# First attention: scores at the end of TensorE's step, the fourth probability copy and the queries on VectorE, GpSimd's step in another order with the lists one step on

## The reference

```python
x = x + cross_attention(n(x), ctx, ctx, mask)   # 16 heads of 16; keys and values from ctx; then layer norm with gamma, beta
x = x + mixture_of_experts(n(x))                # 8 experts, each row goes to its best 2
```

## Time and profile before

| | us |
|---|---|
| median of 3 runs | 970.35 |
| lowest and highest run | 966.97, 971.49 |
| the profiled execution | 968.65 |
| its span, first to last instruction | 966.7 |
| mean granted TensorE clock | 0.971 |
| busy over the span: PE, DVE, ACT, POOL | 863.4, 600.0, 467.1, 391.7 |

### The profile page before, as it was taken

One profiled execution on the slowest core, in us unless ns is written; L12 is line 12 of the kernel. 1 busy time (PEld: TensorE's weight loads), 2 busy tenths in 40 slices (PEclk: granted clock), 3 DMA queues, 4 the chain that ended last, 5 costly groups with the idle time before them and its releaser, 6 DMA issues. The chain is left out here.

```text
span 966.7 us, 26667 instructions
## 1 busy us (share of the span) xinstructions
PE 863.4 (89%) x9044; PEld 729.9 (76%) x9045; DVE 600.0 (62%) x1484; ACT 467.1 (48%) x1194; POOL 391.7 (41%) x610
## 2 busy tenths in 40 slices
PE   4888888759999999998999899999999999779995
PEld 3676776439999999996556588888888887667784
DVE  3587887545555555542027567868668787459995
ACT  3788787412222222222343354445444454459895
POOL 4478886620000000006102346445564545436662
PEclk9999999979999999999999999999999999889998
DMA  6454656342433333316864696777676875212111
GB/s 165 118 164 155 196 159 214 136 165 76 137 95 93 108 95 98 98 35 211 287 197 148 144 180 151 157 148 167 142 158 143 163 157 119 64 41 63 58 59 45
DMA packets 190187, 128.27 MB, mean 133 GB/s; under 512 B 128544, under 2 KB 175648, under 8 KB 189984
## 3 DMA queue, kind: packets, MB, share of 16 engines
q1 hardware_dynamic: 155728, 93.72, 37.5%
q10 hardware_dynamic: 31312, 25.17, 9.1%
q0 software_dynamic: 3072, 8.39, 2.7%
HBM read 78.25 MB, written 48.99 MB: 132 GB/s over the span
## 5 line engine op out<-in xcount | busy, mean ns | idle before, releaser
L1745 ACT ACTIVATE c_pT<-c_T 128x512 f32<-128x512 f32 (+2 forms) x90 | 50.2, 595 | 104.9 <-PE c_T L1904 74.0
L1689 POOL TENSOR_TENSOR c_soft<-c_soft,c_share 128x616 f32<-128x616 f32 (+2 forms) x96 | 70.5, 764 | 63.3 <-DVE c_share L2158 61.8
L1699 POOL MEMSET d_round<- 128x1 f32 x1 | 0.1, 99 | 227.4 <-POOLq L970 227.4
L1080 ACT ACTIVATE b_rowsT<-b_RT 128x256 f32<-128x256 f32 x39 | 15.0, 385 | 157.8 <-PE b_RT L1122 157.8
L1194 DVE COPY b_w<-moe_w 128x1024 f32 x78 | 53.6, 688 | 53.0 <-issue 47.5
L1131 PEld LDWEIGHTS b_G<-b_rowsT,b_w 128*128 128x128 f32 x624 | 77.2, 195 | 4.5 <-DVE b_w L1194 2.4
L1131 PE MATMUL b_G<-b_rowsT,b_w 128*128 128x128 f32 x624 | 77.9, 279 | 1.7 <-DVE b_w L1194 1.1
L1208 DVE SCALAR_TENSOR_TENSOR b_hidT<-b_U,b_bias,b_gate 128x128 f32<-128x128 f32 x156 | 43.9, 344 | 55.6 <-PE b_U L1131 55.6
L1131 PE MATMUL b_U<-b_rowsT,b_w 128*128 128x128 f32 x624 | 76.8, 277 | 0.0
L1158 PE MATMUL b_Y<-moe_w,b_hidT 128*128 x312 | 73.9, 380 | 1.0 <-DVE b_out L1239 1.0
L1131 PEld LDWEIGHTS b_U<-b_rowsT,b_w 128*128 128x128 f32 x624 | 73.6, 194 | 0.0
(11 more groups left out here) (241 smaller groups left out, 2073.1 us busy)
## 6 DMA issues: line engine op xcount, KB each, us to landing
moe_w<-in_L_Wl SPq DMA_DIRECT2D x16, 512.0 KB
rel_windows<-c_relw ACTq DMA_DIRECT2D x28, 276.0 KB, 5.6
c_bias<-rel_windows SPq DMA_DIRECT2D x16, 462.0 KB, 4.9
prob_rows<-c_soft SPq DMA_DIRECT2D x16, 462.0 KB, 5.4
early<-in_L_early SPq DMA_DIRECT2D x16, 384.0 KB, 3.2
values<-c_pT ACTq DMA_DIRECT2D x22, 256.0 KB, 2.6
b_rows<-expert_lists SPq DMA_DIRECT2D x39, 128.0 KB, 2.2
expert_out<-b_out SPq DMA_DIRECT2D x39, 128.0 KB, 1.7
```

The lines of the kernel that those rows point to most:

```text
L1689: ins = nc.gpsimd.tensor_tensor(soft[p][:, hs, a:z], soft[p][:, hs, a:z], share[:, s, hs].unsqueeze(2).to_broadcast([P, HS, z - a]), ALU.mult)
L1745: nc.scalar.activation(dst, view(T[k]), ACT.Copy, **kw).then_inc(g["emptied"], 1)
```

## The change

ScalarE gives two things to VectorE: the query copies with their bias (now one `tensor_scalar` for each of two halves, add then multiply, so the scaled bias `bqs` goes), and the fourth probability copy (`last_probs`, with a semaphore `p3_sb` of its own). TensorE's step is reordered: places and transposes (now of b+1) first, `attention(b-2)` behind probability 0, the scores of b+1 at the end. VectorE's step is reordered too. On GpSimd `both_std` does two deviations in one pair of instructions while both batches exist; listing and scatter are now those of b-4, in the order listing, scatter, and masks come last. From step 16 on `std(2, .)` runs ahead of them.

```diff
-        names = ("... p_mm p_sb pv_mm ...
+        names = ("... p_mm p_sb p3_sb pv_mm ...
+        ALONE = NB - 5
...
+            def both_std(ahead, behind):
+
+                apart(pool, g["var1"], behind + 1)
+                apart(pool, g["var"], ahead + 1)
+                links[0].begin(ahead)
+                links[0](nc.gpsimd.tensor_tensor(rstd[:, 0:2, 0], agg[:, 0:2, 1], eps[:, :], ALU.add))
+                nc.gpsimd.tensor_tensor(rstd[:, 0:2, 1], rstd[:, 0:2, 0], shared["mhalf"][:, :].to_broadcast([P, 2]), ALU.pow)\
+                    .then_inc(g["rstd"], 1)
...
             def steps(b, i, p):
-                if there(b + 3):
+                if there(b + 3) and there(b - 2):
+                    both_std(b + 3, b - 2)
+                elif there(b + 3):
                     std(0, b + 3)
-                if there(b - 2):
+                elif there(b - 2):
                     std(1, b - 2)
-                if there(b + 2):
-                    masks(b + 2, i + 1, p)
-                if there(b - 2):
+                late = isinstance(b, int) and b >= NB
+                if there(b - 2) and late:
+                    std(2, b - 2)
+                if there(b - 4):
+                    listing(b - 4, p)
+                    if there(b - 1):
+                        apart(pool, g["p3_sb"], b)
+                    scatter(b - 4, p)
+                if there(b - 2) and not late:
                     std(2, b - 2)
                 if there(b - 1):
                     residual(b - 1, i - 1 + p, 1 - p)
-                if there(b - 3):
-                    if there(b - 1):
-                        apart(pool, g["p_sb"], 4 * (b - 1) + HPT)
-                    scatter(b - 3, 1 - p)
-                    listing(b - 3, 1 - p)
+                if there(b + 2):
+                    masks(b + 2, i + 1, p)
 
             by_batch(steps)(pool)
+            listing(NB - 1, 1)
+            scatter(NB - 1, 1)
...
ScalarE:
                 if there(b - 1):
-                    for k in range(2):
+                    for k in range(HPT - 1):
                         probs(b - 1, k)
                 if there(b - 3):
                     next_rows(b - 3)
-                if there(b - 1):
-                    for k in range(2, HPT):
-                        probs(b - 1, k)
                 if there(b):
-                    exps(b, p, 0)
-                if there(b + 1):
-                    queries(b + 1, 1 - p)
-                if there(b):
-                    exps(b, p, 1)
+                    for h in range(2):
+                        exps(b, p, h)
...
TensorE, the step after, where there are such batches:
+            places(b - 4), transposes(b + 1), probabilities(b - 1, 0), attention(b - 2), probabilities(b - 1, 1 and 2),
+            next_rows(b - 3), probabilities(b - 1, 3), queries(b + 1), router(b - 3), keys(b + 1), attend(b - 1),
+            values(b + 1), scores(b + 1)
-                if isinstance(b, int) and b >= NB:
-                    text_values(text_halves(b))
                 if isinstance(b, int) and b == NB + 2:
                     places(b - 3, 1 - p)
+                if isinstance(b, int) and b >= NB:
+                    text_values(text_halves(b))
...
VectorE:
+            def queries(b):
...
+                for m in range(KD):
+                    ins = nc.vector.tensor_scalar(qT[:, m, :], M[0][:, m * P:(m + 1) * P], bq[:, m:m + 1], SCALE0, ALU.add, ALU.mult)
+            def last_probs(b):
+                dve.wait_ge(g["p_mm"], 4 * b + HPT)
+                since(dve, g["pv_mm"], b)
+                nc.vector.tensor_copy(pT[HPT - 1][:, :, :], M[1][:, :].rearrange("p (m n) -> p m n", m=MT0)).then_inc(g["p3_sb"], 1)
VectorE, the step after:
+            norm_stats(b + 3), list_rows(b - 4), maxima(b, 0), list_slots(b - 4), denominators(b - 2), rows_normal(b - 3),
+            attention_out, maxima(b, 1), out_rows, last_probs(b - 1), norm_var, out_stats, choose_score, out_var,
+            queries(b + 1), choose_best, keys(b + 1), rows_scaled, choose_index, rows_out, choose_hot, rows_stats,
+            norm_rows(b + 3)
```

More of the change, by code:

```diff
@@ L432, in listing @@
             def listing(b, p):
+                apart(pool, g["slot"], b + 1)
                 nc.gpsimd.tensor_copy(shared["slots"][:, bass.ds(b, 1), :].rearrange("p o k -> p (o k)"), slot_i[p][:, :])
@@ L602, in keys @@
                 pe.wait_ge(g["t_sb"], b + 1)
-                since(pe, g["p_sb"], 4 * (b - 2) + 4)
+                since(pe, g["p3_sb"], b - 1)
                 if isinstance(b, int) and b == 0:
@@ L711, in _ @@
             values(0, 0)
-            transposes(1, 1)
+            scores(0, 0)
             def steps(b, i, p):
+                if there(b - 4):
+                    places(b - 4, p)
+                if there(b + 1):
+                    transposes(b + 1, 1 - p)
+                if there(b - 1):
+                    probabilities(b - 1, 1 - p, 0)
                 if there(b - 2):
                     attention(b - 2)
-                if there(b - 4):
-                    places(b - 4, p)
                 if there(b - 1):
[L720 to L723, removed]
-                    probabilities(b - 1, 1 - p, 1)
+                    for k in (1, 2):
+                        probabilities(b - 1, 1 - p, k)
                 if there(b - 3):
@@ L727, in steps @@
                 if there(b - 1):
-                    for k in range(2, HPT):
-                        probabilities(b - 1, 1 - p, k)
+                    probabilities(b - 1, 1 - p, 3)
+                if there(b + 1):
+                    queries(b + 1, 1 - p)
                 if there(b - 3):
@@ L738, in steps @@
                     values(b + 1, 1 - p)
-                if there(b + 2):
-                    transposes(b + 2, p)
+                    scores(b + 1, 1 - p)
+                if isinstance(b, int) and b == NB + 2:
+                    places(b - 3, 1 - p)
                 if isinstance(b, int) and b >= NB:
                     text_values(text_halves(b))
-                if isinstance(b, int) and b == NB + 2:
-                    places(b - 3, 1 - p)
             by_batch(steps)(pe)
@@ L820, in rows_scaled @@
             def rows_scaled(b):
-                dve.wait_ge(g["rstd1"], b + 1)
+                if there(b + 5):
+                    dve.wait_ge(g["rstd"], b + 6)
+                else:
+                    dve.wait_ge(g["rstd1"], b + 1 - ALONE)
                 return out.add(nc.vector.scalar_tensor_tensor(attf, attf, agg[:, 1, 0:1], gamma[:, :], ALU.subtract, ALU.mult))
@@ L880, in _ @@
             norm_in(1, 0, 1)
+            queries(0)
             dve.wait_ge(s_wk, 32)
@@ L886, in steps @@
             def steps(b, i, p):
-                front, ahead, behind, rows_ready, lists = there(b + 3), there(b + 1), there(b - 2), there(b - 3), there(b - 4)
+                front, ahead, here, past, behind, rows_ready, lists = (there(b + k) for k in (3, 1, 0, -1, -2, -3, -4))
+                if front:
+                    stats = norm_stats(b + 3, i + 1 + p, 1 - p)
+                if lists:
+                    list_rows(b - 4, p)
+                if here:
+                    maxima(b, 0)
+                if lists:
+                    list_slots(b - 4, i - 2, p)
                 if behind:
                     den = denominators(b - 2)
-                if lists:
-                    list_rows(b - 4, p)
                 if rows_ready:
                     rows_normal(b - 3, i - 2 + p, 1 - p)
-                if lists:
-                    list_slots(b - 4, i - 2, p)
-                if front:
-                    stats = norm_stats(b + 3, i + 1 + p, 1 - p)
                 if behind:
                     attention_out(den)
-                if there(b):
-                    maxima(b, 0)
+                if here:
+                    maxima(b, 1)
+                if behind:
+                    rows = out_rows(b - 2, p)
+                if past:
+                    last_probs(b - 1)
                 if front:
                     norm_var(stats)
-                if behind:
-                    rows = out_rows(b - 2, p)
-                if there(b):
-                    maxima(b, 1)
                 if behind:
@@ L913, in steps @@
                     out_var(rows)
-                if front:
-                    norm_rows(b + 3, 1 - p)
+                if ahead:
+                    queries(b + 1)
                 if rows_ready:
@@ L919, in steps @@
                     keys(b + 1, 1 - p)
+                if behind:
+                    rows = rows_scaled(b - 2)
                 if rows_ready:
@@ L922, in steps @@
                 if behind:
-                    rows = rows_scaled(b - 2)
+                    rows_out(b - 2, i - 1, p, rows)
                 if rows_ready:
@@ L926, in steps @@
                 if behind:
-                    rows_out(b - 2, i - 1, p, rows)
                     rows_stats(b - 2, p)
+                if front:
```

(1 more changed line is left out.)

38 lines of the change are left out of this document (16 added, 22 removed).

## The result

| | before | after |
|---|---|---|
| median of 4 runs, us | 969.25 | 997.38 |
| lowest and highest run | 966.97, 971.49 | 986.54, 1001.08 |
| ratio, 95% interval | | 1.027, [1.0232, 1.0308] |
| the profiled execution | 968.65 | 1001.08 |
| its span, mean granted TensorE clock | 966.7, 0.971 | 999.2, 0.951 |

The kernel is 2.7% slower, by 28 us; the forecast was 971.2 us, within 0.5%, and the range ended at 984.

What follows compares the result with a forecast made beforehand. A loop through ScalarE and TensorE was taken to bound the first attention at 10.16 us a step. Early -6, middle -1 and end +9.5 gave +2.5 us on the profiled 968.65: 971.2 us, range 956 to 984.

Steps and rivals of the forecast that it cites:

- What bound the kernel: First attention's batch loop: a loop through ScalarE and TensorE sets 10.16 us a step; no engine is full.
- VectorE's floor: First attention: VectorE's own work per step after the change, with the added copies, forecast at 9.2 us.
- The new wait: In step b, `rows_normal(b-3)` on VectorE must wait until `scatter(b-5)` has landed; forecast turn 10.06 us.
- T = 7.46 + L: Turn from one `rows_normal` to the next: 7.46 us of work and issue plus the store's landing, forecast 10.06 us.
- the term L: Landing time of the second indirect `expert_lists` store, counted from its issue; taken as 2.6 us.
- the quiet row: Earlier profile's landing of 2.5 us, when nothing was loaded behind the experts' weights; the forecast leaned on it.
- Rival 3: At `rows_normal`'s wait, the store loses to weight loads and lands in 3.6 us: about 981 us; chance 0.20.
- the first term: VectorE's part of the turn, from `rows_normal` to the variance, forecast at 3.94 us.
- Rival 4: `norm_rows`, last in VectorE's step, holds up the second store by 0.41 us: 975.3 us; chance 0.10.
- Early: Start and steps 1 to 4, where no store is waited for yet: -6 us (between -4 and -8).
- Middle: Ten steps of the first attention at 10.06 instead of 10.16 us: -1 us (between -3 and +9).
- End: Steps 16 to 18 and last text products, delayed by store waits and last positions: +9.5 us (+4 to +11).

## Why the prediction was wrong

**What bound the kernel** was read rightly. The old loop through ScalarE and TensorE opened: with the reuse wait out of the way (four buffers, or the old order) steps are 9.2 to 9.3 us. **VectorE's floor** of 9.2 us was right in size, 58.5 of 60 us busy with the old order. Whether it binds is open: without the fourth copy the step is as long, but there TensorE waits for ScalarE.

**The new wait** was named at its place, with its rule: `rows_normal` behind the store of b-5, and T = 7.46 + L. It is shown by the four buffers. The sum of its other terms holds where the clock does: with the loads behind the stores a turn less its landing is 7.4 to 8.1 us in the loop, and with TensorE kept busy 7.5 to 7.9.

**The step that failed is the term L.** "I take 2.6: nearer the quiet row." In the loop the landings that `rows_normal` waited for took 4.6 to 6.4 us, 5.1 in the median. The reason given was that mask, context and x loads had moved off; "the first weight load starts within 1 us of the second store" stood in the same sentence and was not priced. Before, weight loads were issued 3.1 to 4.4 us ahead of the second store and its landings spread from 2.4 to 7.3; no row of before showed a store with the weights right behind it, so neither the quiet row nor the median of the earlier trace rows was a bound for it. Rival 3 had the mechanism, the store that loses to the weight loads, but took the median, 3.6, for its price, and so came to 981 us; the kernels whose loads stand elsewhere, 980 and 983 us, are near that, the kernel after is 16 us past it, and past the range. The rule of the Trainium skill (DMA: Bandwidth & Descriptors, "Anatomy of one DMA — SWDGE (gpsimd) path"), 2.3 us by an estimate from its fit, agrees with the undisturbed landings, 2.4 to 2.7 us, and erred by more than the forecast for the loop.

The prediction had the place of the loads, and the diff shows why it is so near. The joint deviation releases two chains at once. In one GpSimd goes through listing to the two stores; in the other VectorE goes through `rows_scaled` and `rows_out`, SyncE stores `x1`, issues two residual loads and then the weights. From the power at 110.65 one takes 3.15 us (113.80) and the other 3.63 (114.28). So the change itself ties the loads to about half a microsecond behind the store in the loop.

**The clock** was not in the sum. A ring with an idle stretch on TensorE longer than before (3.5 us ahead of L667) brings the half clock, and with it 0.9 us of wait into the first term. Where the clock stayed up, that term is shorter than the 3.94 of the forecast: 3.3 to 3.6 us in steps 7 to 11, written out as well as with TensorE kept busy. In these steps of the kernel after it is 4.4 to 4.8. So a term forecast too long hid a part of the clock's price, by luck, and 4.41 for 3.94 looks like a small miss. Pair (1.54 for 1.27) and stores (1.64 for 1.42) make up the other 0.5 us.

**Rival 4** (`norm_rows` holds the second store for 0.41 us) did not come true. The gap between the stores grew by 0.22 us to 1.64, and it is the first store's own row that got longer (1.33 to 1.37 us against 1.11); the issue ahead of the second is 0.30 as before. In step 15 no x is left to norm, so `norm_rows` doesn't run, and the row is as long:

```profile
194.87 1.31 POOL L440 DMA_INDIRECT expert_lists<-a_xn,a_slot  x1 [0.17 <-issue]
196.49 0.98 POOL L440 DMA_INDIRECT expert_lists<-a_xn,a_slot  x1 [0.30 <-issue]
```

What lengthens it is not shown; `rows_out` begins 0.1 us ahead of it, here as in the loop. The rule that rival 4 drew on, that the engine that issues second waits out the other's whole instruction (the Trainium skill, SBUF — State Buffer, "Who interferes with whom"), is neither shown nor refuted here.

**Early**, -6 us was forecast; exponentials(4) start at 55.31 and not 60.04, -4.7, within the bounds of 4 to 8, and the first long landing then takes half of it (-2.3 at exponentials(5)). **Middle**, -1 forecast: from -4.7 to +18.6 at exponentials(15), +23.3. **End**, +9.5 forecast, +12.5 measured: `rows_normal(13)` came 9.78 us after the start of exponentials(15) (8.4 forecast), the gaps were 11.50 and 11.28 (11.0 forecast for both), and the rest behind it grew by 2.3 (1.4 forecast). **Masks last at nothing** was right for the kernel after: from 20 to 200 us the only wait for x is one of 0.9 us, and none is for a mask. It holds because the steps are long: with four buffers and masks last, at 9.2 us a step, x is late three times from 60 to 160 us, by 2.1 us in all; the prediction expected that only under 9 us. **The joint deviation** was costed as 0.9 us off GpSimd, and at nothing in the step; in the kernel after GpSimd waits 31.0 of 100 us, so what it saves there decides nothing. With the old order it is worth 0.6 us a step, 9.3 against 9.9.

What stays open: why landings differ where the loads stand at the same distance (at 0.68 to 0.70 us behind, 2.9 in the kernel after, 3.2 to 4.5 written out and 4.0 to 4.7 in the kernel with the transposes; 2.4 to 7.3 in the kernel before); the two landings of 4.4 and 4.5 us with no weight load near; which of its landings the run of 986.54 us of the kernel after had; and what sets the 9.2 us once the wait is gone.

Four versions beat both kernels: the whole change without GpSimd's new order, 952.75 us (2.0% under the kernel before and 4.5% under the one after), the same with the copy back on ScalarE, 957.19, or with two pairs, 960.63, and the whole change with four row buffers and the loop written out, 957.92 us.

## What to carry over

When a store moves from a place with slack to a place where a buffer's reuse waits for its landing, the landing becomes a term of the step, and it must be priced at the traffic that will stand beside it there: find out which transfers hang on the same event as the store. Before moving anything, count the buffers: more of them cost memory and can take the term out of the ring, as four did here (three were not tried). A wait that leaves TensorE idle for some microseconds costs once more, in the clock of what comes after.

## What was not expected of the hardware

- The same 128 KB indirect store lands in 2.4 to 2.5 us with 768 KB of loads issued 2.3 us behind it, and in 4.6 to 6.4 us with them 0.45 us behind.
- Writing out a loop changed no work and took 17 us off (997.4 to 980.8). What the traces show beside it is some tenths of a microsecond in where SyncE's loads fall, and shorter landings; that the one comes from the other was not tested. The kernel after also spreads more from run to run (986.5 to 1001.1) than any other here.
- A power on two columns (L429, 0.73 us) costs more than one on a single column (0.57 us), but less than two.
